# A macaron block with routed experts: results scattered by adding transfers onto rows that already hold x and half the shared expert

## The chip, the cores and the metric

One core of one Trainium2 chip. The time is the device time of one execution in microseconds (us); lower is better. All operands are float32 in HBM.

## The reference

x is 8192 tokens of width 128 (32 x 256). The block computes

```
x = x + 0.5 * ffn(layernorm(x))
x = x + attn(layernorm(x))
x = x + 0.5 * ffn(layernorm(x))

ffn(x):  shared = (silu(x Gs) * (x Us)) Ds                  # inner width 256
         p = sigmoid(x R + bias); the 2 best of 8 experts, scores divided by their sum
         return shared + sum over the 2 picks of score * (silu(x Ge) * (x Ue)) De
attn(x): q, k, v = x Wq + bq, x Wk, x Wv + bv; q, k scaled, phi = silu + 1, 16 heads of 8
         per sequence of 256: kv = phi(k)^T v;  return (phi(q) kv) Wo + bo
```

## The kernel before, in words

The tokens are cut into 16 tiles of 512 (128 partitions of 4 rows); x stays in SBUF for the whole run. The work has four stages. f is 0 for the first feed-forward part and 1 for the second.

Dispatch (f = 0), to about 176 us: for each tile the norm, a transpose, the router, VectorE's routing (26 small steps a batch, L1392 to L1438), and two copies of the 512 normalised rows, one a pick, each with its number and its weight behind it (520 bytes). GpSimd scatters them (`ffn_tile`, L639): eight indirect transfers of 128 rows a tile into `x_rows` in HBM, sorted by expert. Beside it runs the shared expert: gate and up products, silu on ScalarE (L699), product on VectorE (L1337), down product into `shared_bank` (`down_shared`, L1016), and VectorE's `add_shared` (L1342), which adds half of it to x. VectorE also splits the experts' weights in a high and a low part (L1347) as they are loaded.

Slot stage (f = 0 up to about 370 us, f = 1 from about 575 to 759): 68 slots of 256 rows of one expert. SyncE loads a slot's rows (`load_rows`, L508, six slots ahead) at addresses from tables that VectorE made. TensorE transposes (L1076), computes gate and up in three passes (L924 to L926) and the down product (L1122); ScalarE takes the silu (L825) and copies the expert's weights (L800); VectorE makes the product (L1781) and `slot_results` (L1791, L1793): row numbers, and results times weight into a ring of 12 buffers. GpSimd's `slot_tile` (L651) scatters each slot's results by two indirect transfers of 128 rows of 512 bytes to `y_rows` in HBM, where every token has two rows, one a pick. Rows of padding go behind them, to rows that nobody reads. `load_picks` (L528) loads a tile's two rows a token (512 KB) into one of two buffers `y_pair`, once the scatters of the last slot that can hold a row of that tile have landed (`y_sent`) and the tile two before has been added; VectorE adds them to x by two sums, one in a slot and one in the next (`add_pick`, L1686). For f = 0, eight tiles are added in the slot stage, eight in the turns of the middle.

Middle, 19 turns: attention of tile i, and dispatch for f = 1 with a lag of one to three tiles. `shared_bank` and the attention's output `att_bank` are the same PSUM bank. The turn's order on each engine is written out by hand.

Tail: the last tiles are loaded, added and stored (`store_tile`).

Each engine executes its list in order. SyncE's list holds, in this order for each f: the tables' load, a wait for the scatters of tiles 0 to 11, six slots' rows, eight stores of padding (L544), the next rows, and from slot 17 on rows, picks and stores by place. In dispatch it also loads the experts' weights (L484), each when the one two before has been split; behind the second of them stands the store of all unused padding rows to `x_rows` (L487). GpSimd's list is `ffn_tile` for 16 tiles and `slot_tile` for 68 slots, for f = 0 and then for f = 1:

```
pool.wait_ge(y_to_done, n + 1)
pool.wait_ge(y_out_done, n + 1)
for j in range(JS):
    pool.indirect_dma_start(y_rows, ...y_to[k][:, j:j + 1]..., result_rows(f, s)[:, j, :], None).then_inc(y_sent[k], 16)
```

## Time and profile before

| | us |
|---|---|
| median of 3 runs | 778.35 |
| lowest, highest | 770.6, 781.48 |
| the profiled execution | 780.31 |
| its span | 778.5 |
| TensorE busy | 690.4 (89%) |
| VectorE busy | 552.3 (71%) |
| GpSimd busy | 535.9 (69%) |
| ScalarE busy | 469.2 (60%) |
| median landing of a scatter to y_rows | 2.7 |

PE is TensorE, PEld its weight loads, DVE VectorE, ACT ScalarE, POOL GpSimd, SP or SPq SyncE. L651 is line 651 of the kernel. "<-" stands before what ended a wait; "issue" is time in which the engine waited for nothing that the profile shows. The DMA's transfers themselves are not an engine's busy time; an instruction that issues one on GpSimd is.

### The profile page before, as it was taken

The numbers are of one execution on the slowest core, as the hardware profiler recorded it, in microseconds if no ns is written. First come the engines' busy times: TensorE is split into PE (matmuls) and PEld (weight loads), VectorE is DVE, ScalarE is ACT, GpSimd is POOL, SyncE is SP. The second block draws the span as 40 slices with busy tenths as digits, with TensorE's granted clock in tenths as the row PEclk, the third lists the DMA queues.
The fourth block names the chain that finished last, engine by engine and source line by source line (L and its number), as shares of the span: only waits on it lengthen the run. The fifth ranks groups of instructions, "written<-read, shape, count | busy, mean of one in ns | idle before, by whom it ended". The sixth has DMA issues, their size and how long they took to land.

```text
span 778.5 us, 17599 instructions
## 1 busy us (share of the span) xinstructions
PE 690.4 (89%) x4981; PEld 612.7 (79%) x4981; DVE 552.3 (71%) x1858; ACT 469.2 (60%) x865; POOL 535.9 (69%) x567
## 2 busy tenths in 40 slices
PE   5586867969999999899799999999989999999990
PEld 4466766859999998888566777777769999999990
DVE  6686877886555557767778888877787555567772
ACT  3334534526766776676766767676446766777760
POOL 3474777777777777777257676767777777777773
PEclk8588867989999999999999999999999999999995
DMA  9313221143354345554213211111324354467765
GB/s 279 97 52 121 78 66 49 53 124 107 101 164 132 102 130 152 151 157 137 72 55 95 70 42 43 43 45 46 87 79 122 109 169 115 136 206 227 220 202 171
DMA packets 63445, 89.65 MB, mean 115 GB/s; under 512 B 13174, under 2 KB 43768, under 8 KB 63352
## 3 DMA queue, kind: packets, MB, share of 16 engines
q1 hardware_dynamic: 46456, 53.63, 24.3%
q0 software_dynamic: 16896, 34.90, 13.3%
q8 instruction: 44, 0.72, 0.4%
q14 instruction: 49, 0.40, 0.2%
HBM read 46.36 MB, written 42.12 MB: 114 GB/s over the span
## 4 chain that ended last, share of the span: by engine, by line
PE 61%; DVE 21%; DMA 6%; issue 5%; ACT 2%; SPq 2%; POOL 1%; POOLq 0%; DVEq 0%; ACTq 0%
PE y_bank L1122 12%; PE y_bank L1016 5%; PE g_bank L924 4%; DMA y_pair<-y_rows 4%; PE g_bank L926 4%; PE u_bank L925 4%; PE u_bank L924 4%; PE u_bank L926 4%; PE g_bank L925 4%; PE g_bank L995 3%; PE u_bank L996 3%; PE tr_bank L946 2%; DVE stats L1264 2%; DVE h L1337 2%; PE y_bank L1199 2%
## 5 line engine op out<-in xcount | busy, mean ns | idle before, releaser
L639 POOL DMA_INDIRECT x_rows<-send,send_to x256 | 248.8, 972 | 144.4 <-issue 67.5
L651 POOL DMA_INDIRECT y_rows<-send,y_to x272 | 265.0, 974 | 85.2 <-issue 66.2
L1781 DVE TENSOR_TENSOR h<-silu_g,u_bank 128x512 f32<-128x512 f32 x136 | 93.2, 685 | 110.8 <-ACT silu_g L825 109.2
L800 ACT ACTIVATE slot_gu<-w_gu 128x1024 fp32r x130 | 137.7, 1060 | 40.6 <-issue 36.9
L1122 PE MATMUL y_bank<-w_dn,h 128*128 x1088 | 143.6, 275 | 0.4 <-DVE x L1342 0.4
L1122 PEld LDWEIGHTS y_bank<-w_dn,h 128*128 128x128 f32 x1088 | 132.9, 191 | 0.9 <-issue 0.8
L924 PE MATMUL g_bank<-xT_hi,slot_gu 128*128 128x256 f32 x260 | 84.8, 326 | 14.4 <-DVE xT_lo L1772 13.5
L1016 PEld LDWEIGHTS y_bank<-w_dn,h 128*128 128x128 f32 x512 | 65.3, 202 | 26.9 <-issue 26.2
L825 ACT ACTIVATE silu_g<-g_bank 128x512 f32<-128x512 f32 x136 | 78.9, 580 | 9.7 <-PE g_bank L926 9.6
L1016 PE MATMUL y_bank<-w_dn,h 128*128 128x128 f32 x512 | 66.9, 287 | 16.6 <-DVE x L1342 16.6
L699 ACT ACTIVATE silu_g<-g_bank 128x512 f32<-128x512 f32 x64 | 38.0, 596 | 72.5 <-PE u_bank L926 41.4
L925 PE MATMUL u_bank<-xT_lo,slot_gu 128*128 128x256 f32 x260 | 73.0, 281 | 0.0
L924 PE MATMUL u_bank<-xT_hi,slot_gu 128*128 128x256 f32 x260 | 73.0, 281 | 0.0
L926 PE MATMUL u_bank<-xT_hi,slot_gu 128*128 128x256 f32 x260 | 73.0, 281 | 0.0
L925 PE MATMUL g_bank<-xT_lo,slot_gu 128*128 128x256 f32 x260 | 72.9, 280 | 0.0
L926 PE MATMUL g_bank<-xT_hi,slot_gu 128*128 128x256 f32 x260 | 72.8, 280 | 0.0
L924 PEld LDWEIGHTS g_bank<-xT_hi,slot_gu 128*128 128x128 f32 x260 | 49.2, 189 | 19.9 <-DVE xT_lo L1772 18.1
L1686 DVE TENSOR_TENSOR x<-y_pair,x 128x512 f32<-128x512 f32 x64 | 43.9, 685 | 23.2 <-DMA y_pair<-y_rows 23.0
L711 ACT ACTIVATE send<-x,shift,rstd 128x128 f32<-128x128 f32 x128 | 52.5, 482 | 10.0 <-DVE shift L1304 7.9
L1793 DVE TENSOR_TENSOR send<-y_bank,send 128x256 f32<-128x256 f32 x136 | 56.8, 418 | 0.6 <-PE y_bank L1122 0.3
L925 PEld LDWEIGHTS g_bank<-xT_lo,slot_gu 128*128 128x128 f32 x260 | 49.6, 191 | 0.0
L925 PEld LDWEIGHTS u_bank<-xT_lo,slot_gu 128*128 128x128 f32 x260 | 49.2, 189 | 0.0
(258 smaller groups left out, 1484.0 us busy)
## 6 DMA issues: line engine op xcount, KB each, us to landing
send<-x_rows SPq DMA_DIRECT2D x130, 130.0 KB
y_pair<-y_rows SPq DMA_DIRECT2D x32, 512.0 KB
y_rows<-send,y_to POOLq DMA_INDIRECT x272, 2.7
x<-x_in SPq DMA_DIRECT2D x16, 256.0 KB, 7.2
x_rows<-send,send_to POOLq DMA_INDIRECT x256
out<-x SPq DMA_DIRECT2D x16, 256.0 KB
w_raw<-w_experts SPq DMA_DIRECT2D x15, 256.0 KB, 4.0
x_rows<-pad SPq DMA_DIRECT2D x16, 130.0 KB
```

The source lines that it names most:

```text
L639: pool.indirect_dma_start(x_rows, bass.IndirectOffsetOnAxis(ap=send_to[b % SEND_TO_RING][:, w, k:k + 1], axis=0), send[ring_of(f, t)][:, w ...
L651: pool.indirect_dma_start(y_rows, bass.IndirectOffsetOnAxis(ap=y_to[k][:, j:j + 1], axis=0), result_rows(f, s)[:, j, :], None).then_inc(y_ ...
L711: last = act.activation(send[ring_of(f, t)][:, 0, j, 0:P], x_sub(t, j), ACT.Identity, bias=bias, scale=scale)
L800: act.activation(slot_gu[n % 2][:].rearrange("p a n -> p (a n)"), w_gu[:, bass.ds(e, 1)].rearrange("p e a n -> p (e a n)").bitcast(F32), A ...
L825: act.activation(silu_g[n % 2][:], g_bank[n % 2][:], ACT.Silu).then_inc(slot_silu_done, 1)
L924: pe.matmul(bank_ap, w_parts[0], x_parts[0], start=True, stop=False)
L925: pe.matmul(bank_ap, w_parts[0], x_parts[1], start=False, stop=False)
L926: return pe.matmul(bank_ap, w_parts[1], x_parts[0], start=False, stop=True)
L1016: last = pe.matmul(shared_bank[:, s], h[t % 2][c][:, s], w_dn[:, 0, c, :], start=(c == 0), stop=(c == HALVES - 1))
L1122: last = pe.matmul(y_bank[par][:, j * P:(j + 1) * P], h[par][0][:, c * ROWS + j * P:c * ROWS + (j + 1) * P], w_dn[:, bass.ds(e[j % len(e)] ...
L1781: dve.tensor_tensor(h[par][0][:], silu_g[par][:], u_bank[par][:], ALU.mult).then_inc(slot_h_done, 1)
L1793: dve.tensor_tensor(result_rows(f, s), y_bank[n % 2][:, 0:ROWS].rearrange("p (j d) -> p j d", j=JS), row[:, :, WEIGHT:WEIGHT + 1].to_broad ...
```

## The change

`y_rows` is no longer written by plain scatters. Before them, SyncE stores two 256 KB transfers a tile (`store_base`): x to the rows of the first pick, and half the shared expert to those of the second; the padding rows of `y_rows` are set to 0 once. The scatters add to what is there (`compute_op`), and wait, before slot 0 alone, until all 16 tiles' stores and the zeros have landed. x is then the sum of the two loaded rows: one VectorE sum a tile (`add_picks`) in the place of two, in the slot in which the first was. The shared expert leaves PSUM by ScalarE, times 0.5, into a ring of two buffers (`shared_to_half`), and `add_shared` goes; what waited for it waits for ScalarE. In the middle ScalarE's copy stands one turn later than VectorE's sum did. The stores stand in SyncE's list: for f = 0 behind the weight loads and before and behind the first row loads, the last one behind the padding; the large store to `x_rows` moves from behind the second to behind the third routed expert's weights. The last tile's load of picks for f = 0 moves in between the stores for f = 1. The norms' steps in the slot stage follow one slot earlier.

The diff, cut: left out are the new buffers and semaphores, the renamed waits, the places in the middle where sums are taken out, and unchanged lines.

```diff
@@ -45,6 +45,7 @@
+HALVES_AFTER = {2: (0, 1, 2), 5: (3, 4), 7: (5, 6), 8: (7,)}
@@ -479,13 +482,26 @@
+            def store_base(f, t):
+                sp.wait_ge(shared_halved, f * tiles + t + 1)
+                sp.dma_start(y_tiles[t][:, 0, :], x_tile(t)).then_inc(base_stored[t % 2], 16)
+                sp.dma_start(y_tiles[t][:, 1, :], shared_half[t % 2][:]).then_inc(base_stored[t % 2], 16)
...
-                if e == 2:
+                if e == 3:
...
+                    for b, n in ((0, ROUTED), (ROUTED, PAD_BLOCKS - ROUTED)):
+                        sp.dma_start(y_rows[nobody + b * ROWS:nobody + (b + n) * ROWS].rearrange("(p k) d -> p k d", p=P),
+                                     pad.rearrange("p e j d -> p (e j) d")[:, 0:n * JS, 0:P]).then_inc(nobody_cleared, 16)
+                if e == 2:
+                    sp.wait_ge(x_rest, 16 * (tiles - 4))
+                for t in HALVES_AFTER.get(e, ()):
+                    store_base(0, t)
@@ -521,28 +537,35 @@
-                wait_count(sp, both_added, n - Y_RING + 1)
+                wait_count(sp, picks_added, n - Y_RING + 1)
...
-                sp.wait_ge(both_added, tiles + t + 1)
+                sp.wait_ge(picks_added, tiles + t + 1)
...
+                for t in range(HALVES_AFTER[EXPERTS - 1][-1] + 1 if f == 0 else 0, ROWS_TILE + 2 + (f == 0)):
+                    if f == 1 and t == 1:
+                        load_picks(0, tiles - 1)
+                    store_base(f, t)
...
+                for t in range(ROWS_TILE + 2 + (f == 0), tiles - 1):
+                    store_base(f, t)
...
+                store_base(f, tiles - 1)
@@ -569,7 +592,7 @@
-                    for t in range(len(loads), tiles):
+                    for t in range(len(loads), tiles - 1):
@@ -647,10 +670,14 @@
                 pool.wait_ge(y_out_done, n + 1)
+                if s == 0:
+                    pool.wait_ge(nobody_cleared, 32)
+                    for done in base_stored:
+                        pool.wait_ge(done, (f + 1) * tiles * 16)
                 for j in range(JS):
...
                         y_rows, bass.IndirectOffsetOnAxis(ap=y_to[k][:, j:j + 1], axis=0),
-                        result_rows(f, s)[:, j, :], None).then_inc(y_sent[k], 16)
+                        result_rows(f, s)[:, j, :], None, compute_op=ALU.add).then_inc(y_sent[k], 16)
 
@@ -711,6 +738,13 @@
+            def shared_to_half(f, t):
+                n = f * tiles + t
+                act.wait_ge(shared_psum, n + 1)
+                wait_count(act, base_stored[t % 2], n // 2 * PICKS * 16)
+                act.activation(shared_half[t % 2][:], shared_bank[:], ACT.Copy, scale=0.5).then_inc(shared_halved, 1)
@@ -752,11 +786,14 @@
+                shared_to_half(f, 0)
...
+                shared_to_half(f, 1)
...
+                shared_to_half(f, 2)
@@ -776,9 +813,11 @@
+                    shared_to_half(f, ts[0] - 1)
...
+                        shared_to_half(f, ts[0])
@@ -837,6 +876,8 @@
+                    if s == 0:
+                        shared_to_half(f, tiles - 1)
@@ -885,6 +926,8 @@
+                    if 0 <= i - LAG_G - 2 < tiles - 1:
+                        shared_to_half(1, i - LAG_G - 2)
@@ -1336,11 +1379,6 @@
-            def add_shared(f, t):
-                dve.wait_ge(shared_psum, f * tiles + t + 1)
-                dve.scalar_tensor_tensor(out=x_tile(t), in0=shared_bank[:], scalar=0.5, in1=x_tile(t), op0=ALU.mult,
-                                         op1=ALU.add).then_inc(shared_added, 1)
@@ -1676,14 +1714,12 @@
-            def add_pick(f, t, w):
+            def add_picks(f, t):
...
-                if w == 0:
-                    dve.wait_ge(y_loaded[t % Y_RING], (n // Y_RING + 1) * 16)
-                else:
-                    dve.wait_ge(first_added, n + 1)
-                dve.tensor_tensor(x_tile(t), y_in[t % Y_RING][:, w, :], x_tile(t), ALU.add).then_inc((first_added, both_added)[w], 1)
+                dve.wait_ge(y_loaded[t % Y_RING], (n // Y_RING + 1) * 16)
+                dve.tensor_tensor(x_tile(t), y_in[t % Y_RING][:, 0, :], y_in[t % Y_RING][:, 1, :], ALU.add
+                                  ).then_inc(picks_added, 1)
@@ -1711,15 +1747,12 @@
-                add_shared(f, 0)
...
-                add_shared(f, 1)
...
-                add_shared(f, 2)
@@ -1803,21 +1833,17 @@
-                    if s == 0:
-                        add_shared(f, tiles - 1)
...
-                            add_pick(f, t, 0)
-                        if first_add(f, t) + 1 == s:
-                            add_pick(f, t, 1)
+                            add_picks(f, t)
...
+                            if first_add(f, t) + 1 == s:
+                                normaliser(q, 0, NORM_STEPS // 2)
...
-                                normaliser(q, 0, NORM_STEPS // 2)
-                            if first_add(f, t) + 3 == s:
@@ -1937,9 +1959,8 @@
-                for w in range(PICKS):
-                    if first_add(1, t) + w >= slots:
-                        add_pick(1, t, w)
+                if first_add(1, t) >= slots:
+                    add_picks(1, t)
```

## Rows read from the trace of the kernel before

**Rows 1.** The page: busy time, share and instructions by engine.
```profile
PE 690.4 (89%) x4981; PEld 612.7 (79%) x4981; DVE 552.3 (71%) x1858; ACT 469.2 (60%) x865; POOL 535.9 (69%) x567
```

**Rows 2.** Windows; columns: busy us (instructions) per engine, granted clock, DMA share, GB/s.
```profile
600.00:650.00 50.00, 50.00 (x440) 50.00 (x439) 27.77 (x76) 35.11 (x57) 37.86 (x40) 1.00 0.48 138
700.00:740.00 40.00, 40.00 (x347) 39.55 (x346) 29.89 (x77) 29.54 (x48) 29.64 (x31) 1.00 0.75 220
477.76:490.40 12.64, 12.64 (x78) 9.41 (x78) 9.98 (x41) 9.02 (x20) 9.17 (x10) 1.00 0.13 42
```

**Rows 3.** Chain of waits: start us, us, what; two slots' down products.
```profile
241.87 0.89 PE y_bank L1122 x8
...
244.38 0.89 PE y_bank L1122 x8
```

**Rows 4.** Groups by line, GpSimd; columns: busy us, mean ns, idle before and its releasers.
```profile
L651 POOL DMA_INDIRECT y_rows<-send,y_to x272 | 265.0, 974 | 85.2 <-issue 66.2 <-DVE send L1793 12.7 <-DVE y_to L1791 6.4
...
L639 POOL DMA_INDIRECT x_rows<-send,send_to x256 | 248.8, 972 | 144.4 <-issue 67.5 <-DVE number_weight L1438 39.7 <-DVE send L1449 33.1
...
L591 POOL IOTA phi_q<- 128x1 int32 x1 | 0.2, 227 | 0.0
```

**Rows 5.** Timeline, GpSimd, dispatch: start us, us, engine, line [idle before].
```profile
77.54 0.97 POOL L639 DMA_INDIRECT x_rows<-send,send_to  x1 [9.03 <-DVE number_weight L1438]
...
119.48 0.96 POOL L639 DMA_INDIRECT x_rows<-send,send_to  x1 [1.25 <-DVE number_weight L1438]
```

**Rows 6.** Timeline of VectorE and GpSimd; both scatters: ns min/median/max, first and last start.
```profile
184.08 0.42 DVE L1793 TENSOR_TENSOR send<-y_bank,send 128x256 f32<-128x256 f32 x1
...
364.85 0.42 DVE L1793 TENSOR_TENSOR send<-y_bank,send 128x256 f32<-128x256 f32 x1
...
392.95 0.97 POOL L639 DMA_INDIRECT x_rows<-send,send_to  x1 [17.74 <-DVE send L1449]
...
591.30 0.96 POOL L651 DMA_INDIRECT y_rows<-send,y_to  x1 [0.30 <-issue]
...
L651 POOL DMA_INDIRECT y_rows<-send,y_to x272: 952/963/1482, 201.2 to 766.0; - x136
...
L639 POOL DMA_INDIRECT x_rows<-send,send_to x256: 952/964/1369, 23.5 to 590.0; - x128
```

**Rows 7.** Chain of waits, behind the first slot stage and in the tail.
```profile
371.15 0.69 DVE x L1686
...
769.62 4.84 DMA y_pair<-y_rows
```

**Rows 8.** Groups by line: sums of VectorE; loads of picks (last row, as in rows 6).
```profile
L1686 DVE TENSOR_TENSOR x<-y_pair,x 128x512 f32<-128x512 f32 x64 | 43.9, 685 | 23.2 <-DMA y_pair<-y_rows 23.0
...
L1342 DVE SCALAR_TENSOR_TENSOR x<-y_bank,x 128x512 f32<-128x512 f32 x32 | 21.4, 670 | 10.8 <-PE y_bank L1016 10.8
...
L528 SPq DMA_DIRECT2D y_pair<-y_rows x32: 359/382/392, 285.5 to 769.6; - x32
```

**Rows 9.** Timeline, VectorE, dispatch.
```profile
62.43 0.69 DVE L1342 SCALAR_TENSOR_TENSOR x<-y_bank,x 128x512 f32<-128x512 f32 x1 [0.16 <-PE y_bank L1016]
...
69.05 0.69 DVE L1347 TENSOR_TENSOR w_gu<-w_raw,w_gu 128x512 fp32r<-128x512 f32 x1 [3.98 <-ACT w_gu L666]
```

**Rows 10.** Groups by line, ScalarE: its copy of 128x512 out of PSUM.
```profile
L679 ACT ACTIVATE pad<-tr_bank 128x512 f32<-128x512 f32 x32 | 18.9, 590 | 4.6 <-PE tr_bank L946 4.5
```

**Rows 11.** Timeline of SyncE's queue: stores of padding.
```profile
169.89 8.14 SPq L544 DMA_DIRECT2D x_rows<-pad  x8
...
577.75 8.73 SPq L544 DMA_DIRECT2D x_rows<-pad  x8
```

**Rows 12.** The page: DMA share in 40 slices, and the queues' packets, MB, share.
```profile
DMA  9313221143354345554213211111324354467765
...
q1 hardware_dynamic: 46456, 53.63, 24.3%
...
q0 software_dynamic: 16896, 34.90, 13.3%
```

More of the change, by code:

```diff
@@ L199, in macaron @@
         y_pair = sb("y_pair", [P, 2, PICKS, TT])
+        shared_half = two("shared_half", [P, TT])
         nobody_pad = y_pair.rearrange("p i w n -> p (i w n)")[:, 0:(PAD_BLOCKS - ROUTED) * JS * ROW].rearrange(
@@ L312, in macaron @@
         gu_psum, silu_done, h_done = sem("gu_psum"), sem("silu_done"), sem("h_done")
-        shared_psum, shared_added = sem("shared_psum"), sem("shared_added")
+        shared_psum, shared_halved = sem("shared_psum"), sem("shared_halved")
+        base_stored, nobody_cleared = sems(2, "base_stored"), sem("nobody_cleared")
         rows_loaded, slot_gu_done = sems(ROW_RING, "rows_loaded"), sem("slot_gu_done")
@@ L323, in macaron @@
         y_loaded = sems(Y_RING, "y_loaded")
-        first_added, both_added = sem("first_added"), sem("both_added")
+        picks_added = sem("picks_added")
         proj_psum = sem("proj_psum")
@@ L1009, in down_shared @@
                 pe.wait_ge(h_done, 2 * n + 2)
-                wait_count(pe, shared_added, n)
+                wait_count(pe, shared_halved, n)
                 if f == 1:
@@ L1118, in slot_down @@
                 if s == 0:
-                    pe.wait_ge(shared_added, (f + 1) * tiles)
+                    pe.wait_ge(shared_halved, (f + 1) * tiles)
                 for j in range(JS):
@@ L1192, in attend @@
                 wait_count(pe, x_attended, t)
-                pe.wait_ge(shared_added, tiles + max(0, t - LAG_G - 1))
+                pe.wait_ge(shared_halved, tiles + max(0, t - LAG_G - 1))
                 if t == 0:
@@ L1257, in norm_stats @@
                 if kind == ATTN:
-                    dve.wait_ge(both_added, t + 1)
+                    dve.wait_ge(picks_added, t + 1)
                 if q > 1 and stats_ring(q) < 2:
@@ L1745, in dispatch @@
                         norm(NORM_OF[(FFN, f, BATCHES[f][b + 2][0])][0])
-                    if b > 0:
-                        add_shared(f, ts[0] - 1)
                     if len(ts) > 1:
                         multiply_tile(f, ts[1])
-                        add_shared(f, ts[0])
                     if not ahead:
@@ L1892, in middle @@
                         value(i + 1, 0)
-                    for t in late:
-                        add_pick(0, t, 0)
                     if g:
@@ L1905, in middle @@
                     for t in late:
-                        add_pick(0, t, 1)
+                        add_picks(0, t)
                         norm_stats((ATTN, 1, t))
@@ L1928, in middle @@
                         route(1, i - LAG_T, MASK_STEP, RECIP_STEP)
-                    if 0 <= i - LAG_G - 1 < tiles - 1:
-                        add_shared(1, i - LAG_G - 1)
                     if g and i - LAG_G == tiles - 1:
```

## The prediction

> **What bounds the kernel now.** I read the page's shares and windows by stage first, then GpSimd's groups and timeline, and last the chain and the waits. TensorE looks like the bound: 89% busy, full in two windows of the second slot stage and for 12.64 of 12.64 us in one turn of the middle [rows 1, 2]. In the slot stage the chain passes from one slot's down product to the next in 2.52 us [rows 3]. The share of GpSimd, 69%, hides a second bound. One scatter takes 0.97 us and 0.30 us stand between two of them, labelled "issue", which is no wait for anybody (66.2 us before 216 of the result scatters) [rows 4]: 1.27 us each, two a slot, 2.54 us a slot. So GpSimd needs the same 2.5 us per slot as TensorE. It starts the first stage's result scatters at 201.2, some 17 us after VectorE wrote the first result at 184.1, since the row scatters of dispatch are still in its queue; it ends them at 375.2 (136 x 1.27 = 173 us; the next scatter follows at 392.95 after 17.74 us of idle), 10 us after the last result (365.3); it starts the second stage's at 591.3 and ends at 767.0, with only a few small waits for VectorE [rows 5, 6]. From there the tail runs: landing, load of the last tiles, two VectorE sums, store, 778.5 [rows 7]. The profiled execution took 780.3 us, 1.8 more than its span; the median shown is 778.35, 2.0 less than this execution. I sum against 780.3 and take 2 off at the end.
>
> **What is removed.** VectorE loses 32 sums of the shared expert at 0.67 us and one of two sums of picks a tile, 32 at 0.685 [rows 8]: 43 us of its 552. What is that worth?
> In dispatch, three of these sums, the last at 62.43, stand ahead of the routing of the batch for which GpSimd sits idle 9.03 us until 77.5 [rows 9, 5]: 3 x 0.69 = 2 us. In the same stretch VectorE waits 3.98 us for a weight load that is issued behind the large store of padding rows to x_rows; the change moves that store behind it and puts a 512 KB pair of stores ahead instead: 1 us. With the next idle gap of 1.25 us [rows 5], closed by the later batches' sums, I take 4 us; above it GpSimd works back to back and nothing of dispatch can show. TensorE's waits for the sum of the shared expert go as well, but the first slots' rows need GpSimd's scatters of tile 11 first. Dispatch: -4 us.
> In the middle TensorE is full in every turn; VectorE's 0.67 + 0.69 us are worth nothing there except in the ramp behind the first slot stage, where sums of picks stand on the chain, one at 371.15 [rows 7]: -1 us. In the slot stages nothing is removed but sums beside work; what VectorE waits for there is the load of the picks (23.0 us, 11 times), and that wait stays, since place and ring of the loads stay. In the tail, one sum of 0.7 us goes: -0.7 us.
>
> **What is moved and added.** ScalarE gets 32 copies out of PSUM, 128x512, at 0.59 us (its copies of tr_bank are of that form [rows 10]). In a turn of the middle it is busy 9.02 of 12.65 us [rows 2], so 9.6 fit; behind it in the turn is queued the silu of k, for which VectorE's sum of v waits, while TensorE has other products queued. Cost 0, and 16 x 0.6 = 9.6 us at most if that cover were missing. Over the whole run ScalarE is 60% busy [rows 1].
> SyncE issues 64 stores of 256 KB. Each costs some 0.4 us of its queue and is waited for by nothing until the first adding scatter; where they wait for ScalarE they stand ahead of row loads. Tile 15's pair is issued behind the eight stores of padding, which end at 178.0 and at 586.5 [rows 11]. With 4.8 us for a transfer of 512 KB (tile 15's picks) [rows 7] it lands at about 185 and 592; GpSimd wants to start at 197 and 591.3. Cover in the first stage, at most 1 us lost in the second. The second stage's first six row loads stand behind tile 11's pair, whose half is written in turn 15 of the 19, and the slots start after the last turn. Cost 0.
> The engines of the DMA: 64 x 256 KB = 16.8 MB more; queue 1 moved 53.6 MB in 24.3% of the span (189 us), so 59 us of their time, spread over dispatch and middle, where their share is 0.1 to 0.5 in all but the first slice [rows 12]. Hidden.
>
> **The scatter that adds** replaces 272 plain ones, and here lies the sum. The trace shows no such transfer. Let d be what one costs GpSimd beyond 0.97 us. Not below 0: it does all that a plain one does. Nearest rows: 520-byte rows and 512-byte rows cost the same (972 and 974 ns), and GpSimd's smallest iota takes 0.23 us [rows 4], so some 0.74 us are work for the transfer itself: a list of 128 places to read and one of 128 places to write, and starting the engines. An add must read the target too: a third list. Nothing if that is hidden beside the other two (d = 0), 0.37 if it is half as much again as both, 0.97 if the instruction's time doubles. The nearest row is the plain scatter itself, which pulls towards 0; but nothing shows that the lists are hidden beside each other. I take d = 0.2, near the end of the range at which the nearest row lies and halfway to the half-as-much-again, and keep 0 and 0.97 as ends.
> What does d do? In the second stage GpSimd is in work from end to end but for some 2 us (of the 19.1 us put down to VectorE over both stages [rows 4] most is the usual gap of 0.30): 136 x 0.2 - 2 = +25 us, up to the end. In the first stage GpSimd may fall back further before anybody waits. It ends 10 us behind; a ring of 12 result buffers allows 12 x 2.53 - 2.7 (a scatter's landing, in the table above) = 28 us, but the load of tile 0's picks, issued at 285.5 [rows 8], needs slot 30 landed and is itself wanted 12 slots after that one: 12 x 2.53 - 2.7 - 4.8 = 23, and about 22 is allowed. So 22 - 10 = 12 us are absorbed: 136 x 0.2 - 12 = +15 us. GpSimd's end at 375 + 27 - 4 stands before the middle's first row scatter (17.7 us of idle, shifted by 8), so nothing more there.
> Sum: -4 + 15 - 1 + 25 - 0.7 = +34, 780.3 + 34 = 814, less 2: **812 us**. In general, with d over 0.09: -6 + (136 d - 12) + (136 d - 2).
>
> Two rules of the Trainium skill weigh on d, both apart from the sum. "DMA: Bandwidth & Descriptors", in "Anatomy of one DMA", says that many descriptors can be emitted before the incremental cost shows; by that d is near 0, as the equal rows of 520 and 512 bytes don't contradict (they have equal counts). "Collectives: The Full Stack", in "The bandwidth ceiling", says that a reduce runs at half the rate of a copy, not for the addition but because two sources are read, with two reading descriptors a piece; no row here shows an adding transfer. By it the engines' time for these transfers doubles, and the third list is real.
>
> **Rivals.**
> (B) Adding costs GpSimd nothing or little, d under 0.13. For it: GpSimd's part may be mostly fixed, and the nearest row says so. Against it: one more address a row. Time at d = 0: 780.3 - 6 - 2 = 772; not slower than before, since GpSimd back to back from 77 to 375 and from 559 to 767 lets nothing else through. This is the rival on the other side; it decides at d = 0.13, where the sum is +15.
> (C) Adding is far dearer, d = 0.5 to 0.97, the instruction's time up by half or doubled. 0.5: -6 + 56 + 66 = +116, 894 us. 0.97: -6 + 120 + 130 = +244, 1022 us. (Between it and the forecast stands d = 0.37: -6 + 38 + 48 = +80, 858 us.)
> (D) The DMA engines become the bound though GpSimd doesn't. Queue 0 took 13.3% of the span for 528 transfers, 0.20 us of all engines each; doubled, 272 x 0.2 = 54 us more, 0.15 of the share in the slot stages; in 700 to 740 the share is 0.75 [rows 2, 12], so 0.90 and it holds. Were an add four times a copy, the need would be 0.75 + 0.45 = 1.2 there: the last 60 us stretch by 20%, 12 us, and other stretches at 0.5 hold: about 785 with d = 0.
> (E) The relief of VectorE is worth more than 4 us in dispatch. GpSimd's idle time from its first scatter at 23.5 [rows 6] to 201.2 is 177.7 - 128 x 1.27 = 15 us; all of it gone and d = 0 would give 772 - 11 = 761.
>
> **Chances.** Forecast (d 0.13 to 0.5, slower) 0.39; (B) 0.34; (C) 0.12, slower; (D) 0.07, half of it slower and half within; (E) 0.08, faster. A measurement here tells about 2%, 15.6 us, from no change: slower 0.39 + 0.12 + 0.03 = 0.54, within 0.34 + 0.04 = 0.38, faster 0.08. The forecast's own range is 794 to 894. The range that holds 8 in 10 reaches from 768, just under B, to 900, d = 0.52.
>
> **What would show it.** Duration of the y_rows scatter on GpSimd, 0.97 before: 1.17 by the forecast, 0.97 by B. The time from the first to the last of them in the second stage, 175.7 us: 203 by the forecast. Its last start in the first stage relative to its first, 173: 200. TensorE's slots 2.52 apart in the first third of a stage and near 2 x 1.47 = 2.94 at the end of the second, with VectorE waiting for landed scatters, which it never did. The 9.03 us gap of GpSimd 3 us shorter. The middle's turn 12.64 as before. Wrong would be a scatter of unchanged length with a longer time (then D, or a wait that I missed: tile 15's stores), or a shorter kernel by over 10 us (then dispatch was worth more).

## The result: 917 us, slower by 18%

The kernel after the change takes 916.87 us (median of 4 runs, 916.73 to 918.75), the kernel before 777.37 beside it: a ratio of 1.1806, with a 95% interval of 1.1752 to 1.186. The forecast was 812 with a range of 768 to 900. The time is above the range, and the sign was called right.

The page of the kernel after; the first row answers to [rows 1], the queues' to [rows 12], and the last gives the shares of the chain that ended last, by engine.

```profile
PE 714.1 (78%) x4981; PEld 629.7 (69%) x4981; DVE 517.9 (56%) x1794; ACT 488.8 (53%) x897; POOL 697.2 (76%) x567
...
q0 software_dynamic: 47360, 34.90, 26.9%
q1 hardware_dynamic: 59544, 72.38, 26.1%
...
PE 20%; POOL 15%; issue 6%; DMA 4%; SPq 2%; DVE 2%; ACT 1%; POOLq 0%; ACTq 0%; DVEq 0%
```

VectorE's instructions, added up by groups, lost 42 us, as forecast (its busy time, in which overlapping instructions count once, fell by 34), and ScalarE gained 20. GpSimd gained 161 us with the same 567 instructions. The chain of waits of this kernel can be followed back only to 452 us, so its shares sum to 50%, and they can't be set against those of the kernel before; in the half that it covers GpSimd holds 15 of the 50.

GpSimd's group and its source line in the kernel after (durations in ns, least, median and most; first and last start), to be read against [rows 4, 6]:

```profile
L678 POOL DMA_INDIRECT y_rows<-send,y_to x272 | 425.8, 1565 | 85.9 <-issue 76.2 <-DVE y_to L1821 3.4 <-DMA y_rows<-shared_half 3.2
L662 POOL DMA_INDIRECT x_rows<-send,send_to x256 | 249.3, 974 | 121.7 <-issue 72.4 <-DVE number_weight L1476 31.3 <-DVE send L1487 15.0
...
L678 POOL DMA_INDIRECT y_rows<-send,y_to x272: 1552/1553/2017, 200.1 to 904.5; - x136
```

One adding scatter holds GpSimd for 1.565 us where a plain one held it for 0.974: d is 0.59 us. The scatters to x_rows, which are still plain, take 0.974 (0.972 before), so it is the form and not GpSimd as a whole. With the unchanged pause of 0.30 the cycle is 1.86 us, 3.73 a slot, against TensorE's 2.51 [rows 3]. It is back to back at both ends of the first stage and into the middle (timeline of GpSimd, kernel after):

```profile
200.06 1.62 POOL L678 DMA_INDIRECT y_rows<-send,y_to  x1 [0.30 <-DVE send L1823]
201.98 1.59 POOL L678 DMA_INDIRECT y_rows<-send,y_to  x1 [0.30 <-issue]
...
452.38 1.56 POOL L678 DMA_INDIRECT y_rows<-send,y_to  x1 [0.30 <-issue]
454.24 0.99 POOL L662 DMA_INDIRECT x_rows<-send,send_to  x1 [0.30 <-issue]
...
651.84 1.61 POOL L678 DMA_INDIRECT y_rows<-send,y_to  x1 [3.23 <-DMA y_rows<-shared_half]
```

Laid beside [rows 6], GpSimd's list alone accounts for all of the 138.4 us between the two spans:

| place in GpSimd's list | before | after | later by |
|---|---|---|---|
| first result scatter | 201.2 | 200.1 | -1.1 |
| end of the first stage's | 375.2 | 453.9 | 78.7 |
| the middle's first row scatter | 392.95 | 454.24 | 61.3 |
| second stage's first result scatter | 591.3 | 651.84 | 60.5 |
| end of the last one | 767.0 | 906.1 | 139.1 |
| end of the span | 778.5 | 916.9 | 138.4 |

Each stage costs 79 to 80 us, which is 136 x 0.59. The idle 17.74 us ahead of the middle takes up 17.4 of the first; the second is paid in full. The idle time of 3.23 us before the second stage's first scatter, of which 0.30 is the usual pause, is a price of the new stores and not of the adding form.

The other engines wait for GpSimd. Groups of VectorE in the kernel after, and the longest wait of TensorE between 730 and 782 us (us in total, times, longest):

```profile
L1821 DVE CAST y_to<-send 128x2 int32<-128x2 f32 x136 | 26.3, 194 | 92.3 <-DMA y_rows<-send,y_to 92.3
...
L1721 DVE TENSOR_TENSOR x<-y_pair 128x512 f32<-128x512 f32 x32 | 21.9, 686 | 42.1 <-DMA y_pair<-y_rows 42.1
...
PE route_bank L1119 <- DMA send<-x_rows: 31.5, 1, 31.5
```

The first row is the full ring of 12: VectorE may not write new row numbers before an old scatter has landed. In the kernel before VectorE never waited for that. 79.2 of the 92.3 us fall in the first stage (200 to 450 us), 13.1 behind it. The second row is the one sum a tile that replaced [rows 8]'s two. The third is what stops TensorE in the second stage: it stands still for 31.5 us until a slot's rows are loaded. SyncE has that load behind a load of picks, and the picks have to wait for scatters to land, which GpSimd now issues later (SyncE's queue, kernel after):

```profile
703.61 28.98 SPq L524 DMA_DIRECT2D send<-x_rows  x11
768.59 0.39 SPq L544 DMA_DIRECT2D y_pair<-y_rows  x1
770.23 2.55 SPq L524 DMA_DIRECT2D send<-x_rows  x3
```

GpSimd had results of earlier slots to scatter all that time, so this stop is another place where TensorE waits for GpSimd, and no cost of its own. Windows of the kernel after: a turn of the middle, the same 12.64 us as in [rows 2], and then the second stage. TensorE starts full, stops, catches up and is short of work again. Its granted clock was at 1.00 in [rows 2]; here it is 0.56 and 0.50 (its lower level, 1.2 GHz) in the stretches without a matmul, and 1.00 again from 780 to 825 us.

```profile
535.71:548.35 12.64, 12.64 (x78) 9.42 (x78) 9.29 (x40) 9.51 (x21) 8.20 (x10) 1.00 0.24 82
650.00:700.00 50.00, 49.59 (x431) 49.15 (x430) 30.54 (x89) 35.29 (x57) 40.43 (x26) 1.00 0.69 119
700.00:750.00 50.00, 39.52 (x337) 38.38 (x336) 22.07 (x60) 28.32 (x44) 41.87 (x27) 0.97 0.55 76
745.00:765.00 20.00, 0.00 (x0) 0.00 (x0) 0.49 (x2) 0.00 (x0) 16.87 (x11) 0.56 0.40 36
765.00:772.00 7.00, 0.00 (x0) 0.00 (x0) 0.00 (x0) 0.00 (x0) 5.86 (x4) 0.50 0.64 105
780.00:825.00 45.00, 43.72 (x374) 42.74 (x373) 27.74 (x74) 31.99 (x52) 37.74 (x24) 1.00 0.92 204
850.00:900.00 50.00, 21.35 (x141) 20.59 (x139) 12.22 (x31) 10.23 (x16) 42.07 (x27) 0.70 0.60 99
```

GpSimd is busy 84% of each of the windows of the second stage from 700 us on (42 of 50 us, 27 x 1.56), at a DMA share of 0.40 as at one of 0.92: it is saturated, with its fixed pauses.

### The profile page after: what moved, and what is told of

It reads as the page before. It is cut to its first block, busy times and chain, and to the rows that moved or that the text cites. A ratio compares the mean times of both kernels' runs of the same rounds, so it can differ in the third digit from the quotient of the medians.

```text
span 916.9 us, 17666 instructions
## 1 busy us (share of the span) xinstructions
PE 714.1 (78%) x4981; PEld 629.7 (69%) x4981; DVE 517.9 (56%) x1794; ACT 488.8 (53%) x897; POOL 697.2 (76%) x567
## 3 DMA queue, kind: packets, MB, share of 16 engines
q0 software_dynamic: 47360, 34.90, 26.9%
## 4 chain that ended last, share of the span: by engine, by line
PE 20%; POOL 15%; issue 6%; DMA 4%; SPq 2%; DVE 2%; ACT 1%; POOLq 0%; ACTq 0%; DVEq 0%
POOL y_rows L678 13%; PE g_bank L1038 3%; PE u_bank L1039 2%; PE y_bank L1059 2%; DMA send<-x_rows 2%; POOL x_rows L662 1%; PE y_bank L1165 1%; DMA y_rows<-send,y_to 1%; PE y_bank L1242 1%; PE route_bank L1010 1%; PE g_bank L1206 1%; PE y_bank L1222 1%; PE tr_bank L989 1%; PE u_bank L1206 1%; PE u_bank L1212 1%
## 5 line engine op out<-in xcount | busy, mean ns | idle before, releaser
L678 POOL DMA_INDIRECT y_rows<-send,y_to x272 | 425.8, 1565 | 85.9 <-issue 76.2
L1165 PE MATMUL y_bank<-w_dn,h 128*128 x1088 | 149.7, 282 | 0.1
L1165 PEld LDWEIGHTS y_bank<-w_dn,h 128*128 128x128 f32 x1088 | 138.9, 199 | 0.8 <-issue 0.5
L967 PE MATMUL g_bank<-xT_hi,slot_gu 128*128 128x256 f32 x260 | 87.5, 337 | 50.4 <-DVE xT_lo L1802 50.2
L1821 DVE CAST y_to<-send 128x2 int32<-128x2 f32 x136 | 26.3, 194 | 92.3 <-DMA y_rows<-send,y_to 92.3
L968 PE MATMUL u_bank<-xT_lo,slot_gu 128*128 128x256 f32 x260 | 74.9, 288 | 0.0
L969 PE MATMUL u_bank<-xT_hi,slot_gu 128*128 128x256 f32 x260 | 74.9, 288 | 0.0
L967 PE MATMUL u_bank<-xT_hi,slot_gu 128*128 128x256 f32 x260 | 74.8, 288 | 0.0
L969 PE MATMUL g_bank<-xT_hi,slot_gu 128*128 128x256 f32 x260 | 74.5, 286 | 0.0
L1059 PEld LDWEIGHTS y_bank<-w_dn,h 128*128 128x128 f32 x512 | 63.8, 197 | 8.6 <-issue 7.2
L847 ACT ACTIVATE xT_hi<-route_bank 128x256 fp32r<-128x256 f32 x62 | 23.8, 384 | 79.1 <-PE route_bank L1119 79.0
L1059 PE MATMUL y_bank<-w_dn,h 128*128 128x128 f32 x512 | 63.9, 279 | 0.0
L847 ACT ACTIVATE xT_hi<-tr_bank 128x256 fp32r<-128x256 f32 x68 | 26.1, 384 | 62.8 <-PE tr_bank L1119 62.3
```

Source lines behind the costliest of these rows:

```text
L678: pool.indirect_dma_start(y_rows, bass.IndirectOffsetOnAxis(ap=y_to[k][:, j:j + 1], axis=0), result_rows(f, s)[:, j, :], None, compute_op= ...
L967: pe.matmul(bank_ap, w_parts[0], x_parts[0], start=True, stop=False)
L968: pe.matmul(bank_ap, w_parts[0], x_parts[1], start=False, stop=False)
L969: return pe.matmul(bank_ap, w_parts[1], x_parts[0], start=False, stop=True)
L1059: last = pe.matmul(shared_bank[:, s], h[t % 2][c][:, s], w_dn[:, 0, c, :], start=(c == 0), stop=(c == HALVES - 1))
L1165: last = pe.matmul(y_bank[par][:, j * P:(j + 1) * P], h[par][0][:, c * ROWS + j * P:c * ROWS + (j + 1) * P], w_dn[:, bass.ds(e[j % len(e)] ...
```

## The experiments

The theory: the adding form holds GpSimd longer, and the time follows the cycle of GpSimd and nothing else. The rivals: the transfers themselves (the engines of the DMA, 64 stores more), the new places and waits of the change, and, within the theory, what an adding scatter's length depends on. All runs but the last four were made beside the kernel before at 776 us.

**The change without the adding.** All stores, waits, copies and moved sums stay; one argument goes.

```diff
-    result_rows(f, s)[:, j, :], None, compute_op=ALU.add).then_inc(y_sent[k], 16)
+    result_rows(f, s)[:, j, :], None).then_inc(y_sent[k], 16)
```

> Edit: the changed kernel with the addition taken out of the result scatters, everything else of the change kept (stores of x and of half the shared expert, ScalarE's copy, one sum a tile). Left out: x and the shared expert's half don't reach the result. Theory 1 (GpSimd's instruction time decides: 272 scatters at 1.565 instead of 0.974 us): scatters back at 0.97 us, the rest of the change is worth -2 to -6 us, so 771 to 776 us. Rival 2 (the added traffic and the stores' waits carry a part of the +139 us): stays above 800 us.

Measured: 770.96, ratio 0.9941 (0.9908 to 0.9974). The adding form is worth 146 us, all the rest of the change -5. GpSimd's groups, its timeline ahead of the middle, and queue 0 of this kernel's page:

```profile
L678 POOL DMA_INDIRECT y_rows<-send,y_to x272 | 263.6, 969 | 86.5 <-issue 66.2 <-DVE send L1823 15.7 <-DVE y_to L1821 4.6
...
78.43 0.97 POOL L662 DMA_INDIRECT x_rows<-send,send_to  x1 [8.86 <-DVE number_weight L1476]
...
386.66 0.96 POOL L662 DMA_INDIRECT x_rows<-send,send_to  x1 [11.85 <-DVE send L1487]
...
q0 software_dynamic: 16896, 34.90, 13.5%
```

The -5 doesn't come from dispatch, whose gap is 8.86 us against 9.03 [rows 5]. The profiled executions, 767.9 and 778.5 us long, are 10.6 apart: 6.3 of it stands at the middle's first row scatter (386.66 against 392.95), and 3.5 in the second stage's scatters, 171.2 us from first to last start against 174.7. The first of these varies: in two later kernels with a plain first stage that scatter starts at 387.60 (`compute_op` in the second stage alone) and at 390.71 (without the stores). So the ramp behind the first stage is worth 2 to 6 us.

**GpSimd held longer without any adding.** The kernel before, with a memset by GpSimd behind each result scatter: no transfer, store or wait of the change is in it.

```diff
+    m = 2 * n + j
+    wait_count(pool, idle_done, m)
+    pool.memset(idle_cols[:], 0.0).then_inc(idle_done, 1)
```

> Edit: the kernel before, with a GpSimd memset of 128x600 behind each result scatter, on a tile that nobody reads; no adding transfer, no new DMA, no new wait for another engine. It lengthens GpSimd's cycle by some 0.55 to 0.6 us a scatter, as the addition did. Theory 1: 0.57 x 272 - 14 (what is absorbed) = +141, so 905 to 925 us. Rival 2 (DMA side: 9 packets an engine instead of 2, landing 3.3 instead of 2.7 us): near 780 us.

Measured with 600 columns: 888.38, ratio 1.1438 (1.1371 to 1.1505), below what was expected. The timeline of GpSimd shows why: the pause shrinks from 0.30 to 0.17 us behind a memset, so the cycle is 1.75 and d is 0.48, not 0.6.

```profile
299.55 0.97 POOL L652 DMA_INDIRECT y_rows<-send,y_to  x1 [0.17 <-issue]
300.52 0.61 POOL L657 MEMSET idle_cols<- 128x600 f32 x1
301.30 0.97 POOL L652 DMA_INDIRECT y_rows<-send,y_to  x1 [0.17 <-issue]
```

With 300 and with 150 columns:

```diff
-        idle_cols = sb("idle_cols", [P, 600])
+        idle_cols = sb("idle_cols", [P, 300])
```

> Edit: memset_before with 300 columns instead of 600. There the cycle of GpSimd was 1.75 us a scatter (0.48 more than 1.27) and the time 888. A memset of 300 columns takes 0.27 us less: cycle 1.48, d = 0.21, the size that the prediction took for the addition. By its formula without the change's gains: (136 x 0.21 - 12) + (136 x 0.21 - 2) = +43, 820 us. If the first stage absorbs more than 12 us: under 812.

> Edit: memset_before with 150 columns: cycle about 1.35 us, d = 0.08. By the formula the first stage absorbs all of its 11 us and the second shows 136 x 0.08 - 2 = +9: 786 us. If both stages are bound by GpSimd from end to end: +22, 799 us.

Measured: 820.25, ratio 1.0562 (1.0503 to 1.0621), and 795.22, ratio 1.0248 (1.0189 to 1.0308). The first is what was expected. The second lies between the two numbers named for it, 786 and 799, nearer to the rival's: the pause was 0.16 to 0.17, so d is 0.115. (The profiled executions, 791.9 and 778.5 us long, differ by 13.4 only.) Timeline with 300 columns, a cycle of 1.50:

```profile
301.15 0.97 POOL L652 DMA_INDIRECT y_rows<-send,y_to  x1 [0.17 <-issue]
302.13 0.36 POOL L657 MEMSET idle_cols<- 128x300 f32 x1
302.65 0.97 POOL L652 DMA_INDIRECT y_rows<-send,y_to  x1 [0.17 <-issue]
```

All lie within some 5 us of one line: (136 d - 17.4), or 0 where that is less than 0, for the first stage, whose delay the idle time ahead of the middle takes up, and (136 d - 2) for the second. The 17.4 was read from the kernel with the change, so the last row is no test of it; the memset rows are:

| kernel | d | by the line | measured |
|---|---|---|---|
| 150 columns | 0.115 | +14 (second stage alone) | +19 |
| 300 columns | 0.235 | +45 | +44 |
| 600 columns | 0.48 | +111 | +112 |
| the change | 0.59 | +141 | +140 |

The change, with 19 MB more through queue 1 and 30,000 more packets in queue 0, stands on the line of kernels that have none of it. The line leaves out the 5 us that the rest of the change saves; counted from the kernel without the adding, with its shorter idle time of 11.85 us, the sum is (80.2 - 11.85) + (80.2 - 2) = 147, where 146 were measured. The price is the engine's time.

**One stage at a time.** `compute_op` only where f is 0, and only where f is 1.

> Edit: the changed kernel with adding scatters for the first feed-forward part alone, plain ones for the second (there x and the shared expert's half don't reach the result). Theory 1 by the formula of the prediction with d = 0.59 and a dispatch gain of 1 instead of 4 us: -3 + (136 x 0.59 - 12) = +65, 842 us. If the first stage's delay were mostly absorbed by the middle: under 820. If the stages don't add up: not the rest of 139 against the next run.

> Edit: the changed kernel with plain scatters for the first feed-forward part (x and the shared expert's half are lost there), adding ones for the second. Theory 1: -3 + (136 x 0.59 - 2) = +75, 852 us. Together with the run before the two sum to the +139 of the changed kernel plus one time -3 to -6.

Measured: 838.54, ratio 1.08 (1.0737 to 1.0862), and 851.69, ratio 1.0973 (1.0902 to 1.1043), both within 4 us of what was expected. Over the 770.96 of the kernel without adding that is 67.6 and 80.7. The first stage costs less by 13.1. What it can hide in is the idle time ahead of the middle, which is 11.85 us in the trace of the kernel without adding and 16.55 in that of the kernel with a plain first stage alone; the parts sum to 148 where both together measure 146.

**What the length depends on.** A slot in four each of 128 rows adding, 64 adding, 128 plain and 64 plain.

```diff
+    if s % 4 == 0:   ...y_to[k][:, j:j + 1]..., result_rows(f, s)[:, j, :], None, compute_op=ALU.add
+    elif s % 4 == 1: ...y_to[k][0:half, j:j + 1]..., result_rows(f, s)[0:half, j, :], None, compute_op=ALU.add
+    elif s % 4 == 2: ...y_to[k][:, j:j + 1]..., result_rows(f, s)[:, j, :], None
+    else:            ...y_to[k][0:half, j:j + 1]..., result_rows(f, s)[0:half, j, :], None
```

> Edit: the changed kernel with four forms of the result scatter in turn by slot: 128 rows adding, 64 rows adding, 128 rows plain, 64 rows plain (half of the rows of half of the slots are left out, and plain rows overwrite x or the shared half). Theory 1a (the third list costs by the row): the added time halves with the rows, 64 adding minus 64 plain = 0.30 us. Theory 1b (a fixed cost of the adding form): the difference stays 0.59 us. Rival 2 (the instruction is long because queues are full or memory is slow behind it): the adding form's minimum isn't constant.

Groups of GpSimd, in that order (830.26 us, one execution):

```profile
L680 POOL DMA_INDIRECT y_rows<-send,y_to x68 | 109.6, 1612 | 23.6 <-issue 18.0 <-DMA y_rows<-shared_half 3.2 <-DVE y_to L1835 1.2
L684 POOL DMA_INDIRECT y_rows<-send,y_to x68 | 97.8, 1438 | 20.7 <-issue 19.2 <-DVE send L1837 1.5
L688 POOL DMA_INDIRECT y_rows<-send,y_to x68 | 66.9, 983 | 20.8 <-issue 18.6 <-DVE send L1837 1.5 <-DVE y_to L1835 0.6
L692 POOL DMA_INDIRECT y_rows<-send,y_to x68 | 62.4, 918 | 20.7 <-issue 18.9 <-DVE send L1837 1.2 <-DVE y_to L1835 0.6
```

In this mixture the 128-row forms take 1.612 and 0.983 us, 0.05 and 0.01 more than in the kernels with one form. 64 rows fewer save 0.065 us on the plain form (1.0 ns a row) and 0.174 on the adding one (2.7 ns a row). Adding costs 0.63 us at 128 rows and 0.52 at 64, so by a straight line some 0.41 of it don't depend on the rows at all (an estimate; nothing between or below 64 was run). The 0.52 fits neither theory exactly, and is nearer to the fixed 0.59 than to the 0.30. Rival 2 fails: in the kernel with the change the adding form's least time, 1.552, and its median, 1.553, are the same (the L678 row above). The picture of "a third list" as long as the others is wrong: neither form's time is mostly its rows.

**The stores.** In the kernel without adding, also the 64 stores of x and half the shared expert taken out, with the waits for them.

```diff
-    sp.dma_start(y_tiles[t][:, 0, :], x_tile(t)).then_inc(base_stored[t % 2], 16)
-    sp.dma_start(y_tiles[t][:, 1, :], shared_half[t % 2][:]).then_inc(base_stored[t % 2], 16)
...
-    for done in base_stored:
-        pool.wait_ge(done, (f + 1) * tiles * 16)
```

> Edit: plain_after without the 64 stores of x and of half the shared expert, their waits on GpSimd and ScalarE gone (x and the shared expert's half don't reach the result). Theory 1: the stores are hidden, 771 us as plain_after within 3 us. Rival 2: several us less, by what the 16.8 MB cost.

Measured: 768.75, ratio 0.9883 (0.9829 to 0.9936), against 0.9941 (0.9908 to 0.9974) with them. The ratios differ by 0.0058, 4.5 us, the medians by 2.2, and the intervals overlap: the stores cost less than 10 us, and a cost isn't shown.

**Two that didn't tell what they were made for.** One-column memsets behind all 528 scatters of the kernel before; and, in the kernel without adding, ScalarE's copy of tile 2's shared half moved behind the next tiles' work in its list (the last of the expectations calls it sums of VectorE; the edit is this one).

```diff
+    m = (f * tiles + t) * PICKS * SUB + w * SUB + j
+    pool.memset(short[:, m:m + 1], 0.0)
...
+    m = 2 * tiles * PICKS * SUB + n * JS + j
+    pool.memset(short[:, m:m + 1], 0.0)
```

```diff
-                shared_to_half(f, 2)
                 send_normalised(f, 6)
                 high((FFN, f, 5))
                 send_normalised(f, 7)
+                shared_to_half(f, 2)
```

> Edit: the kernel before, with a memset of one column behind each of the 528 scatters, each to a column of its own. In the memset runs the gap before a scatter was 0.16 to 0.17 us where a memset stood ahead of it, 0.30 where a scatter did, and the scatter took 0.98. With a memset of 0.10 us the cycle would be 0.98 + 0.10 + 0.16 = 1.24 instead of 1.27 us. If GpSimd bounds the kernel before: 528 x 0.03 = 16 us of its time, of which some 8 to 10 lie where it works back to back: 766 to 770, faster. Rival (GpSimd's work adds up, the gap doesn't shrink for so short an instruction): cycle 1.37 us, +15 to 20, 795 us.

> Edit: plain_after with ScalarE's copy of the shared expert's half of tile 2 moved behind the high part of tile 5 and the sends of tiles 6 and 7. In plain_after ScalarE waits 2.85 us for TensorE at that copy, and VectorE 4.77 us for the high part behind it. Theory: VectorE's wait falls to about 1 us and GpSimd's gap before the batch of tiles 4 and 5 from 8.9 to 6 us, so that its result scatters start at 198 instead of 201; the time 1 to 3 us less than plain_after, 768 to 770. Rival: the weight load, now issued later, takes the wait's place and the gap stays near 9.

> The kernel before with a memset of one column by GpSimd behind each of the 528 scatters; the same kernel as short_memsets, to be compared with a kernel of before near 777 us if the chip gives that. The memset runs measured a cycle of a scatter of 1.385 us with 150 columns and 1.505 with 300; with one column the cycle was 1.28 us in the profile of short_memsets, against 1.27 in that of before. Theory 1 (the time follows the cycle of GpSimd and nothing else, the pause between two scatters takes up the short memset): within 4 us of before, ratio 0.995 to 1.005. Rival (any added instruction costs its own 0.1 us, as the pauses are those of the issue): 528 x 0.11 = 58 us less what the two dips absorb, a ratio of 1.02 or more.

> The kernel of plain_after (scatters plain, so x and half the shared expert are left out of the result) with the second half of the shared expert's sums moved behind the sends of groups 6 and 7. The same kernel as half_later. Theory 1 (the half-expert work of VectorE ahead of the dispatch's last sends is what keeps the dispatch gap at 8.5 to 8.9 us instead of the 5 to 6 that were forecast): the gap falls to about 6 us and the time to about 768. Rival (the gap is set by the sends themselves): gap 8.5 or more, the time 770 to 773 as in plain_after, or above if the later sums hold up the first store.

These four ran on chips where the kernel before took 987.89 us (first pair) and 1005.62 (second), and they are compared only with that. Measured for the memsets: 1000.45, ratio 1.0161 (1.0103 to 1.022), then 1011.27, ratio 1.0033 (0.9988 to 1.0079), two intervals that don't meet. For the moved copy: 991.08, ratio 1.0021 (0.9987 to 1.0056), then 1008.57, ratio 1.0025 (0.999 to 1.0061): no difference from before, and the predicted drop of the gap can't be read, since GpSimd there waits 20 us for VectorE where it waited 9. The trace of its first run, set against that of the kernel without adding on its faster chip, shows both sides of the question: VectorE's wait for the transpose's copy fell from 4.77 us to 1.32, as the theory has it, and its waits for the weights grew from 1.51 + 1.55 to 1.99 + 2.47, as the rival has it. On these chips GpSimd isn't back to back (group of GpSimd, second run of the moved copy):

```profile
L678 POOL DMA_INDIRECT y_rows<-send,y_to x272 | 263.0, 967 | 239.0 <-DVE send L1823 135.2 <-issue 83.8 <-DMA y_rows<-shared_half 17.1
```

So neither question is answered as to time. What the first run of the memsets still shows is a cycle (GpSimd's timeline):

```profile
404.25 0.11 POOL L658 MEMSET short<- 128x1 f32 x1
404.55 0.97 POOL L654 DMA_INDIRECT y_rows<-send,y_to  x1 [0.19 <-issue]
405.52 0.11 POOL L658 MEMSET short<- 128x1 f32 x1
405.83 0.97 POOL L654 DMA_INDIRECT y_rows<-send,y_to  x1 [0.19 <-issue]
```

404.55 to 405.83 is 1.28 us with the memset inside, against 1.27 without: in the pause of 0.30 us behind a scatter another instruction can run.

## Where the prediction was right, and where it was wrong

**The bound was right.** That GpSimd paces the slot stages beside TensorE, hidden behind a busy share of 69%, is what the memset kernels show: 0.12 us more a scatter already costs 19 us. The law "-6 + (136 d - 12) + (136 d - 2)" gives, with the measured d of 0.59, -6 + 68 + 78 = +140, and 780.3 + 140 - 2 = 918, against 917 measured.

**What failed is one term: the size of d.** "I take d = 0.2" measured 0.59, and so the sum's +34 us measured +140. 0.2 was put near zero because the nearest row was the plain scatter, and 0.37 and 0.97 came from a picture of lists, one a side. The forms show that the picture has no hold: the rows are a small part of the instruction (1.0 ns each of 0.98 us), and most of what adding costs doesn't depend on them. No row of the trace before could have given 0.59. It lay inside the bounds of 0 and 0.97, and the case C, "d = 0.5 to 0.97", held it with a chance of 0.12. Given bounds that far apart and a slope of 272 us for each us of d, the chance for the upper half was too small, and the range's upper end of 900 stood for d = 0.52, hardly past the middle of the bounds.

**The case of B, d = 0, was run as the kernel without the adding.** The forecast for it was 772, and 770.96 was measured. So the terms besides d were right in sum, but in part by luck, as their errors cancel:
- "Dispatch: -4 us" measured about -1: the gap of 9.03 is 8.49 in the kernel after, and the result scatters start at 200.1. The three sums did go, but VectorE starts the same weight split at the same time, 68.89 against 69.05. The new wait is one that I hadn't looked for: tile 2's shared half stands in ScalarE's list ahead of a transpose's copy, waits 2.81 us for the down product, and VectorE waits for that copy. By this VectorE's split of an earlier expert's weights ends late, at 65.52; SyncE issues the next weight load only then, at 65.55 (63.75 in the kernel before), and the split at 68.89 needs that load. Timeline of the kernel after, ScalarE, VectorE and SyncE:

```profile
61.28 0.60 ACT L747 ACTIVATE shared_half<-y_bank 128x512 f32<-128x512 f32 x1 [2.81 <-PE y_bank L1059]
...
63.32 0.58 ACT L708 ACTIVATE xT_hi<-tr_bank 128x512 fp32r<-128x512 f32 x1
...
63.93 0.69 DVE L1374 TENSOR_TENSOR xT_lo<-tr_bank,xT_hi 128x512 fp32r<-128x512 f32 x1 [4.73 <-ACT xT_hi L708]
...
64.84 0.68 DVE L1385 TENSOR_TENSOR w_gu<-w_raw,w_gu 128x512 fp32r<-128x512 f32 x1
...
65.55 0.33 SPq L493 DMA_DIRECT2D w_raw<-w_experts  x1
...
68.22 0.63 ACT L693 ACTIVATE w_gu<-w_raw 128x512 fp32r<-128x512 f32 x1 [1.23 <-DMA w_raw<-w_experts]
```

  The forecast costed ScalarE's copies in a turn of the middle, where they are indeed free, and not in dispatch, where the list is another. Whether moving this copy would give the 3 us back was tried, but not on a chip that could show it: it stays argued. The trace of that run speaks against all of the 3, since SyncE has the weight load behind the stores that wait for the moved copy: the copy ended at 74.70 us and the load was issued at 75.57.
- The ramp, "-1", was worth more: -2 to -6 at the middle's first row scatter, by three traces. The two misses nearly cancel.
- The stores of tile 15 in the second stage, "at most 1 us lost": GpSimd stands idle 3.23 for them, 2.9 more than its usual pause. GpSimd was free for its first result scatter at 648.9, and SyncE had just issued that pair, at 647.72 and 648.21, behind eight stores of padding (its queue, kernel after):

```profile
639.48 8.19 SPq L566 DMA_DIRECT2D x_rows<-pad  x8
647.72 0.45 SPq L488 DMA_DIRECT2D y_rows<-x  x1
648.21 0.45 SPq L489 DMA_DIRECT2D y_rows<-shared_half  x1
```

**"The first stage absorbs 12" and "nothing more there" for the middle were two errors that cancelled.** I counted the fall-back that the rings allow, 22 us, in slots of TensorE's 2.53 us. But a ring that is full moves at GpSimd's pace: 12 x 3.73 - 3.3 = 41. In the trace VectorE writes the stage's last result at 410.76 and GpSimd ends at 453.94, 43 us behind. So VectorE's last result came 46 us later than before (364.85, [rows 6]), where the law gives 68: the stage itself lost less than I said; and the middle lost the rest, its first row scatter being 61 us later, because its first work stands behind those scatters in GpSimd's list. Waits of the kernel after, 440 to 470; columns: us in total, times, longest.

```profile
PEld g_bank L1038 <- DVE h L1380: 12.7, 1, 12.7
PE g_bank L1038 <- DVE h L1380: 12.6, 1, 12.6
DVE shift L1363 <- POOL rstd L651: 12.4, 1, 12.4
ACT send L738 <- DVE shift L1363: 11.6, 1, 11.6
```

What absorbs is therefore the idle time in GpSimd's list ahead of the middle: 17.74 us in the kernel before, and 11.85 to 16.55 in three traces of kernels with this change and a plain first stage. That it is near the 12 that I had from the rings is luck.

**D, the DMA as the bound, was wrong, though its condition nearly held.** Queue 0 took 13.3% of 778.5 = 103.5 us of all engines' time before and 26.9% of 916.9 = 246.6 after: 143 us for 272 adding scatters, so 0.53 more than a plain one's 0.20. An adding scatter takes the engines 0.72 us, 3.7 times a copy; the forecast's case was four times. It came near its limit in one stretch: the share is 0.92 from 780 to 825 us, where TensorE catches up and rows, picks and stores of x fall together. But GpSimd went on issuing every 1.86 us there and TensorE was busy 43.72 of 45 us, so it bound neither; elsewhere the share is 0.24 to 0.69 in the windows shown. The Trainium skill, "Collectives: The Full Stack", "The bandwidth ceiling", has a reduce at half the rate of a copy, as two sources are read; the page says this of rings between ranks and gives its model for no other case. Carried over to this scatter the factor would be 2; here it is 3.7, and the measurement decides. Of the other rule ("DMA: Bandwidth & Descriptors", "Anatomy of one DMA": many descriptors before the incremental cost shows) the forms agree as to rows, with 0.065 us for 64 more; drawing from it that d is near 0 was my mistake, since a change of form isn't a change of count.

**E, all 15 us of GpSimd's idle time in dispatch gone, did not happen:** the gap stayed.

**One reading was incomplete.** What holds the slots apart besides GpSimd is SyncE's list, in which row loads stand behind loads of picks. The forecast had the slots spread evenly as GpSimd lags; in the second stage they came in bursts, with TensorE idle for 31.5 us in one piece. (Also, [rows 3] give 2.51 us a slot and not 2.52; nothing hangs on it.)

What was to show the forecast right: the middle's turn is 12.64 us as said; TensorE starts the second stage full and ends it waiting, and VectorE waits for landed scatters, as said; GpSimd's slots are 3.73 us apart in the place of 2.94; from the start of the second stage's first scatter to the end of its last there are 254.3 us, where 203 was forecast.

## What to carry to other kernels

Where an engine issues transfers back to back, its instruction's time and its pause, times the count, is a bound beside the busy shares, and every change to the instruction's form is multiplied by the whole count: measure one such instruction before building on it. Where its price is unknown and its slope is large, give the bounds the chance that they have, not the nearest row. And count what a list absorbs in that list, up to its next idle gap, at the pace of the engine that lags.

Here, a version that adds in HBM would have had to save more than 146 us elsewhere; it saved 5. No kernel run here computes the whole block faster than the kernel before.

## What the runs showed of the hardware

- An indirect scatter that adds, 128 rows of 512 bytes, holds GpSimd 1.565 us against 0.97 plain. In the kernel that mixes the forms it is 1.61 against 0.98, and 1.44 against 0.92 at 64 rows.
- It goes out in more packets: (47360 - 256 x 32) / 272 = 144 each against 32, 9 an engine against 2, for the same bytes. It lands in 3.3 us where the plain one landed in 2.7 (medians), and takes the engines 0.72 us against 0.20.
- The pause of GpSimd behind a scatter is 0.30 us before another scatter, and 0.16 to 0.19 between a memset that fills part of it and the next scatter.
- TensorE's granted clock was 0.50 in a stretch of 7 us without a matmul that followed 20 such us at 0.56, and 1.00 again in the 45 us from 780 on.
- The same kernel before took 776, 988 and 1006 us on different chips. The slower ones were profiled with other kernels alone: there GpSimd's scatters still took 0.97 us, TensorE was busy 761 to 764 us where it was 684 to 690 with the same instructions, at a mean granted clock of 0.87 to 0.88 in the place of 0.94 to 0.95, and the engines waited longer for each other. What causes that is not known here.
